# Results of the last stage: one indirect scatter of 128 rows a tile from GpSimd, in place of four transfers a group from the sync queue

## What is computed

```python
hidden_after_attn = hidden_states + proj_out
x = layernorm(hidden_after_attn)                       # ln2
top_probs, top_idx = top_k(softmax(x @ router_weight.T), 2)
h_mid = gelu(einsum('th,ehf->etf', x, moe_w1))         # 8 experts, 256 inner features
expert_out = einsum('etf,efh->eth', h_mid, moe_w2)
return hidden_after_attn + sum_e expert_out[e] * weight[e]
```

## Time and profile before

| | us |
|---|---|
| median of 3 runs | 865.34 (865.15 to 866.01) |
| span of the profiled execution | 862.7 |
| median of the runs less the span | 2.6 |
| TensorE busy | 727.4 (84% of the span) |
| VectorE busy | 639.6 (74%) |
| ScalarE busy | 408.4 (47%) |
| GpSimd busy | 198.2 (23%) |
| first TensorE work of the last stage, from the span's start | 648.88 |

### The profile page before, as it was taken

One profiled execution on the slowest core, in us unless ns is written; L12 is line 12 of the kernel. 1 busy time (PEld: TensorE's weight loads), 2 busy tenths in 40 slices (PEclk: granted clock), 3 DMA queues, 4 the chain that ended last, 5 costly groups with the idle time before them and its releaser, 6 DMA issues. The chain is left out here.

```text
span 862.7 us, 26300 instructions
## 1 busy us (share of the span) xinstructions
PE 727.4 (84%) x10112; PEld 545.5 (63%) x10112; DVE 639.6 (74%) x1802; ACT 408.4 (47%) x777; POOL 198.2 (23%) x317
## 2 busy tenths in 40 slices
PE   3468898888888889889999477887759999999997
PEld 2245565555556777667787245665547888888886
DVE  7568877787868989888996577887665766666653
ACT  3123223322235656656655365665635555554553
POOL 3333222232534212330200553342011110011100
PEclk9569989998898999999999599999998999999999
DMA  4000000140034221122200000000000000000000
GB/s 103 9 22 13 23 21 21 33 88 18 24 99 100 82 78 50 53 66 79 81 15 14 4 2 5 5 4 4 5 3 2 13 13 0 12 12 12 12 13 13
DMA packets 33082, 26.43 MB, mean 31 GB/s; under 512 B 9740, under 2 KB 29912, under 8 KB 32984
## 3 DMA queue, kind: packets, MB, share of 16 engines
q1 hardware_dynamic: 29944, 24.07, 10.5%
q10 hardware_dynamic: 3040, 0.98, 0.5%
HBM read 13.51 MB, written 7.34 MB: 24 GB/s over the span
## 5 line engine op out<-in xcount | busy, mean ns | idle before, releaser
L1931 PEld LDWEIGHTS bank<-w2r,hme 128*128 128x128 f32 x1024 | 132.2, 191 | 15.6 <-ACT hme L1876 1.4
L1931 PE MATMUL bank<-w2r,hme 128*128 128x128 f32 x1024 | 135.5, 276 | 0.0
L1876 ACT ACTIVATE hme<-bank,b 128x512 f32<-128x512 f32 x128 | 86.5, 687 | 96.3 <-PE bank L97 96.3
L984 ACT ACTIVATE P<-bank 128x512 f32<-128x512 f32 x128 | 76.6, 598 | 76.2 <-PE bank L1130 75.0
L1900 DVE SCALAR_TENSOR_TENSOR Xq<-bank,wgte,Xq 128x128 f32 (+1 forms) x256 | 72.1, 344 | 51.1 <-PE bank L1931 38.3
L1056 DVE TENSOR_SCALAR bank<-bank 128x512 f32<-128x512 f32 x128 | 89.6, 700 | 15.2 <-PE bank L1121 14.4
L1064 DVE TENSOR_REDUCE mx<-bank 128x4 f32<-128x512 f32 x128 | 87.1, 681 | 1.4 <-PE bank L1104 1.3
L500 ACT ACTIVATE w2r<-bank 128x512 f32<-128x512 f32 x40 | 23.9, 597 | 114.5 <-PE bank L814 82.8
L1130 PE MATMUL bank<-mT,negsel 128*128 128x128 f16 x512 | 51.0, 223 | 13.9 <-DVE bank L1056 12.6
L95 PE MATMUL bank<-xTe,w 128*128 (+1 forms) x128 | 48.8, 381 | 5.5 <-PEq L1295 5.5
L825 PE MATMUL bank<-w_raw,hm 128*128 128x128 f32 x320 | 50.3, 308 | 2.9 <-DVE X L739 2.8
(11 more groups left out here) (382 smaller groups left out, 1785.3 us busy)
## 6 DMA issues: line engine op xcount, KB each, us to landing
cross_q<-qh SPq DMA_DIRECT2D x24, 128.0 KB
Q<-cross_q SPq DMA_DIRECT2D x8, 384.0 KB, 3.9
X<-in_x SPq DMA_DIRECT2D x8, 256.0 KB, 2.8
Xq<-X SPq DMA_DIRECT2D x32, 64.0 KB
cross_k<-kh SPq DMA_DIRECT2D x16, 128.0 KB
Yq<-Y SPq DMA_DIRECT2D x32, 64.0 KB
out_x<-Xq SPq DMA_DIRECT2D x32, 64.0 KB, 1.7
cload<-in_ctx SPq DMA_DIRECT2D x8, 192.0 KB, 2.5
```

The lines of the kernel that those rows point to most:

```text
L984: act.activation(P[j][:], TB[u % 3][:], ACT.Exp, scale=SCALE).then_inc(s["p_ready"], 1)
L1876: act.activation(hm[:, p % HR], UP[p % RING][:], ACT.Gelu_apprx_tanh, bias=b1[:, p:p + 1]).then_inc(s["gelu"], 1)
L1931: last = pe.matmul(Y[f % 2][:, cols], hm[:, p % HR, cols], w2r[:, p], start=(p % 2 == 0 and i == 0), stop=(p % 2 == 1), skip_group_check=True)
```

## The change

The index table `rows` is new: a [128, 32] tile of unsigned integers, where row (p, n) holds the number of the output row, 128 b' + 32 i + n. GpSimd fills it with four iotas at the head of its stream of the last stage, each waited for. The sync engine issues nothing in the stage any more and only waits for all of the stores. For each of the four n of a group GpSimd issues one indirect DMA, which writes the 128 partitions' rows of 512 bytes to the 128 output rows that `rows[:, n]` names. GpSimd's stream is written out for all groups instead of using the hardware loop. In it the stores of group g - 1 stand at step 10 of group g, which in this stream means behind the residual sum of group g + 1; those of the last group stand at the end.

```diff
+        "rows": sb("rows", [128, S // 4], mybir.dt.uint32),
...
+    rows, rows_out = e["rows"], out.rearrange("b s c -> (b s) c")
...
-            for g in range(G):
-                sp.wait_ge(s["x4_ready"], g + 1)
-                for i in range(4):
-                    at = 32 * i + GB * g
-                    sp.dma_start(out[:, at:at + GB, :], X3[32 * i:32 * i + 32, GB * g:GB * g + GB, :]
-                                 ).then_inc(s["stored"], 16)
-            sp.wait_ge(s["stored"], 16 * 4 * G)
+            sp.wait_ge(s["stored"], 16 * GB * G)
...
                     if nxt(g) and p == 9:
                         expert_sum(pool, e, X3, H, g + 1)
-            over_rest(pool, step, G - 1)
+                    if g > 0 and p == 10:
+                        store(g - 1)
+                if g == G - 1:
+                    store(g)
+
+            def store(g):
+
+                pool.wait_ge(s["x4_ready"], g + 1)
+                for n in range(GB * g, GB * g + GB):
+                    pool.indirect_dma_start(out=rows_out, out_offset=bass.IndirectOffsetOnAxis(ap=rows[:, n:n + 1], axis=0),
+                                            in_=X3[:, n, :], in_offset=None).then_inc(s["stored"], 16)
+            for i in range(4):
+                pool.iota(rows[32 * i:32 * i + 32, :], pattern=[[1, S // 4]], base=32 * i, channel_multiplier=S
+                          ).then_inc(s["rows_ready"], 1)
+                pool.wait_ge(s["rows_ready"], i + 1)
+            for g in range(G):
+                step(g)
```

More of the change, by code:

```diff
@@ L1689, in expert_state @@
         rs_e r_ready xn_e xT_e_psum xTe_hi xTe_lo lg_psum g_in g_exp g_step wgt_ready up_psum gelu
-        down_psum x4_step x4_ready stored carrier4""")
+        down_psum x4_step x4_ready stored rows_ready carrier4""")
     return e
```

## The result

| | us |
|---|---|
| before, median of 6 runs | 865.67 (864.42 to 867.41) |
| after, median of 6 runs | 870.01 (867.84 to 871.64) |
| ratio after to before | 1.0048, 95% interval 1.0031 to 1.0065 |
| span of the profiled execution, before and after | 862.7 and 867.0 |

The kernel became slower by 0.48%, 4.3 us; forecast were 3.8 us and 869.1.

A forecast was written before the change was run, and what follows sets the result against it. TensorE fills the last stage's full groups; only the 3.48 us behind the last combine are unhidden. Issuing 3.35, landing 0.4 and signal 0.1 make 3.8 us on 865.34, so 869.1 us, range 866.4 to 874.0.

The forecast's parts named there:

- The place: Last stage: stores before the last group cost 0 us; the whole price lies behind VectorE's last combine, hidden by nothing.
- T = 1.27 us: Last group: price of one GpSimd scatter, from near GpSimd rows; four take 5.08 us against 1.73, so +3.35 us.
- The signal: Last group: GpSimd starts 0.09 us after the releasing VectorE instruction, the sync queue after 0.02; +0.1 us.
- The landing: Behind the last issue: counted from a scatter's end instead of an issue's start; +0.4 us, bounds 0 and +2.0.
- The closing: End of the block, after the stores have landed: 0.45 us in the kernel before, with no change added.
- the last combine at 859.2: Sign in the trace: VectorE's last combine ends there as before; another time would mean the stage itself has moved.
- The middle: Seven groups before the last: 0 us, scatters covered by idle GpSimd with 23.6 us of room before its next root.
- The index table: Head of GpSimd's block: four iotas, 0.8 to 1.6 us in all, hidden before GpSimd's first work; 0 us.
- The port: GpSimd beside VectorE: shared ports may slow the normalise while scatters run; no change behind the last combine, without VectorE work.
- the rival in which the normalise waits behind scatters: Six middle groups: VectorE's normalise delayed, TensorE stalled 1.9 to 2.2 us a group; 880 to 882 us; chance 0.09.
- The rival "no slower": Behind the last combine: scatters issue about as fast as transfers, under 0.73 us each; 866.1 us at 0.5; chance 0.12.
- The rival of long scatters: Behind the last combine: a scatter takes 2 to 3.5 us, adding 6.3 to 12.3 plus landing; 872 to 878; chance 0.07.

The follow-up runs named there:

- last_by_sync: Changed kernel with the last group's stores back on the sync queue, groups 0 to 6 still by scatter; ratio to the kernel before 0.9998.
- last_by_scatter: Changed kernel with groups 0 to 6 stored by the sync queue and only the last group by four scatters; ratio to the kernel before 1.0039.
- half_scatter: Changed kernel with each scatter cut into two of 64 rows, eight a group; a single execution took 875.86 us.
- wide_scatter: Changed kernel with one scatter a group, 128 rows of 2,048 bytes, instead of four; ratio to the kernel before 1.000.
- early_drain: Changed kernel with one GpSimd drain added in idle time between the scatters of group 6 and group 7; ratio to the kernel before 1.0038.
- crowd: Changed kernel with 20 more scatters a group into spare memory in groups 0 to 5; a single execution took 906.55 us.
- plain_gpsimd: Changed kernel with GpSimd issuing the sync queue's four plain transfers a group instead of scatters; ratio to the kernel before 1.0023.

## Why the prediction was right, step by step

- **The place** was right: nothing in the middle of the stage, everything behind the last combine. Shown by last_by_sync (0.9998) and last_by_scatter (1.0039).
- **T = 1.27 us** was right as a distance between scatters (1.26), but by luck, for the near rows have nothing to do with it: it is a nearly fixed price of the indirect form (half_scatter, wide_scatter), and a plain transfer by GpSimd takes 0.50. The term was 3.35 us and measured 3.01 (4.74 less 1.73), because the gap of 0.30 behind the last scatter is not paid.
- **The signal**: +0.1 was forecast, +0.26 measured (0.28 from the end of the combine to the first scatter, 0.02 to the sync queue's first transfer).
- **The landing**: +0.4 was forecast, 0 measured: 1.3 us behind the last issue's end, before and after. Counted from an instruction's start the median is 2.3 us instead of 1.7, which the longer instruction accounts for.
- **The closing** is the step that failed. The prediction carried it as 0.45 us unchanged. GpSimd's drain became the last to end, 1.35 us behind the landing; it puts 1.2 us on the tail, and early_drain took them away again. The sum, 3.8 against 4.4, was near because errors cancelled in part: the issuing was 0.34 too high, the landing 0.4 too high, the signal 0.16 too low, and this term of 1.2 was missing. The range had no place for it and covered it only by its bounds for the issuing and the landing. It was luck too that the 1.37 us by which the profiled stage began earlier and the 1.23 by which it ran longer nearly met; the prediction took the last combine at 859.2 as a sign that the stage had not moved.
- **The middle**: 0 us was right (181.10 and 181.09 us, above). The wait for the combine was met when it was reached, the root still waited for VectorE, and the cover of 23.6 us was real: crowd exhausts it and pays.
- **The index table**: four iotas of 148 ns, 0.80 us together, at the lower end of the estimate of 0.8 to 1.6; GpSimd then idled for 4.30 us until its first root.
- **The port**: the rival in which the normalise waits behind scatters did not come. The normalise shows 334/335/1285 ns (333/336/1285 in the earlier trace rows); what gave way was the scatter. The first one of a group, beside the normalise, takes 1.10 us, the same in the last two groups, with no normalise beside it, 0.96:

```profile
708.17 1.10 POOL L1872 DMA_INDIRECT out_x<-Xq,rows  x1 [0.18 <-issue]
...
836.03 0.96 POOL L1872 DMA_INDIRECT out_x<-Xq,rows  x1 [18.35 <-DVE Xq L1913]
```

That these 0.14 us are the port's is argued from this pairing, not tested: the slow scatters are also the ones that follow a compute instruction of GpSimd directly. Against that reason speak four of the 120 spare scatters of crowd, which follow another scatter and took 1.03 to 1.21 us. Each lay beside VectorE's comparisons of 128x256 (698.03, 765.40, 797.13 and 830.29), but others lay beside them too and took 0.96 (731.21), so the rule is open. A scatter that gives way beside the normalise is the direction that the Trainium skill, "SBUF — State Buffer", Who interferes with whom, gives for descriptors that GpSimd writes beside a tensor_scalar.
- **The rival "no slower"** fell with T. It would have held for plain transfers only as far as the issuing goes; with their drain they are slower too (1.0023). The rival of long scatters, 2 us and more, fell with T as well.

## What to carry to other kernels

The stores of the last group stand behind everything else, so what counts there is how long the instructions take that issue them and how the block closes; the 28 like them before cost nothing on any engine that has room. A scatter's price is nearly fixed: if four rows of the index table name four neighbouring rows of the output, one wide scatter does the work of four. And when GpSimd issues transfers, its drain at the end of the block can be what ends last: let another engine issue the last ones (last_by_sync, tail 3.43 us), or drain once in idle time ahead of them (early_drain, 6.72 instead of 7.92).

## What the runs showed of the hardware that was not expected

- GpSimd's drain ends later the more it has issued since its last drain, up to 32 transfers: 1.5 us behind the last instruction after 4, 2.7 after 32; it was 5.3 after 64 smaller ones and 4.3 after 152. A drain with no transfers ahead of it ended with its last instruction (before: 810.8 + 2.08 = 812.9, the sum through at 812.8).
- An indirect scatter takes 0.96 us for 128 rows, of 512 or of 2,048 bytes, and 0.89 for 64 rows, with 0.30 us behind each. The first transfer of a program that GpSimd issues takes 0.27 us more (last_by_scatter 1.23 us, plain_gpsimd 0.77). A plain transfer by GpSimd takes 0.50 us and has no gap.
- The four scatters leave the DMA engines mostly idle (share at most 0.39 in any half microsecond of the changed kernel's tail); in the wide scatter the same bytes go through in one burst of about 1 us:

```profile
860.50:861.00 0.50, 0.00 (x0) 0.00 (x0) 0.00 (x0) 0.00 (x0) 0.00 (x0) 0.85 0.83 319
861.00:861.50 0.50, 0.00 (x0) 0.00 (x0) 0.00 (x0) 0.00 (x0) 0.00 (x0) 0.50 0.54 205
```
- A store written as one transfer for a whole group lands in 5.8 us (859.3 to 865.1) instead of 3.1 for four transfers (859.24 to 862.3), at a DMA share of about a quarter.
